# A post-norm decoder layer on one core: the first block's rows are stored as f16 parts and come back transposed by a DMA, where TensorE transposed them before

## The chip, the cores and the metric

The kernel runs on one core of a Trainium2 chip. The metric is the device time of one launch in microseconds (us), the median of three runs. The core has five engines that run side by side and meet only at semaphores: TensorE (PE in the rows; PEld is its weight load), VectorE (DVE), ScalarE (ACT), GpSimd (POOL), and SyncE (SP), which here does nothing but issue DMAs. SP's DMAs all go onto one DMA queue, q1.

## The reference

Sixteen sequences of 112 rows and 1024 columns pass through three blocks; each is `layernorm(x + block(x))`.

```python
# self-attention, head size 256, biases on q, k, v and the output
qkv = einsum('bsc,cf->bsf', x, Wqkv) + bqkv
x = layernorm(x + softmax(q @ k.T / 16) @ v @ Wo + bo)                # called x1 below
# cross-attention over ctx (375 rows of 1024 for each sequence)
Q = x @ Wq.T + bq;  K = ctx @ Wk.T + bk
x = layernorm(x + softmax(Q @ K.T / 32) @ ctx)                        # x2
# feed-forward, 2752 wide, weights packed in 4 bits and unpacked with scales and zeros
x = layernorm(x + (silu(x @ Wg) * (x @ Wu)) @ Wd)
```

## The kernel before

**Precision.** An f32 operand of a large product is split into an f16 high part and an f16 rest, and the product is three f16 products (high x high, high x rest, rest x high). Splitting takes two instructions: ACT writes the scaled high part, and DVE writes "scaled value minus high part".

**Stages.** The 16 sequences (n, in code also m) go in 4 groups (g) of GB = 4 (b is the place in a group).

*Self-attention, 33 to about 250 us.* For each group PE makes the four q/k products (index f), which ACT copies out in order (L1083; banks 2 and 3 in turn, so f + 2 cannot start before f is copied), then values, scores and, after the softmax, the output product of each sequence. DVE adds the residual (L482), takes the statistics (L376, L379, L381), waits for POOL's inverse deviation (L950), and applies the norm (L386), which signals `s_n`. SP stores each finished row tile `yo[b % 2]` as x1 (L1707) and loads the residual rows of the sequence two further on (L1705); POOL adds the output bias to these (L959), a step that stands in its queue just ahead of the inverse deviation of the sequence before. This run of norms lies beside the next group's q/k products on PE. DVE begins the next group with a maximum over its input (L401) and, in groups 1 and 2, with a block of small table instructions, ahead of the softmax. `xtp` holds a group's transposed input in f16 parts.

*Weights of the cross-attention, about 240 to 354 us.* Wq and Wk are multiplied in f32, in eight chunks of some 13.7 us on PE (`m_chunk`). ACT copies each out (L1124) and, just ahead, issues the load of the Wq columns of the chunk after next. Beside the last two chunks stand the x1 transposes of group 0: `x1_transposed(m, b, bank)` loads nothing itself; it takes row tiles that SP and ACT loaded back from x1 into `xs3`, makes eight f32 transposes of 112x128 into two banks (L1385), and `x1t_hi` on ACT (L1132) and `x1t_lo` on DVE (L645) write two f16 parts of them each into `xtp`.

*Cross-attention, 390 to 745 us.* One pass of a loop per sequence n on PE: logits (112x375) with a quarter of the g products (`g_chunk`: x1 times the combined weight, for the pair of sequences after this one), context transposes (L1457), softmax transposes (L1475), another quarter, the attended product, the last quarter, the x1 transposes of sequence n + 4 (L1385), and the transposes of the finished x2 rows of n - 1 (L1490). Each quarter is copied twice by ACT (L1139, L1143) and split by POOL (L1024); the logits of an even n wait for the last of these splits. The first quarter after the logits of an odd n waits for `s_x1l`, the end of `x1t_lo`.

*Feed-forward, 745 to 1977 us.* Not touched.

Each engine's order is written out by hand, with `Fori` loops over groups; `Fori(1, NG - 1)` runs groups 1 and 2, groups 0 and 3 stand outside.

## Time and profile before

| | |
|---|---|
| median of 3 runs | 1975.22 us (1974.12 to 1978.18) |
| the profiled execution | 1978.52 us, of which the span from first to last instruction is 1976.8 us |
| PE | busy 1889.8 us (96% of the span), 11238 matmuls |
| DVE, ACT, POOL | busy 880.5 us (45%), 476.2 us (24%), 320.3 us (16%) |
| granted TensorE clock | mean 0.988 of 2.4 GHz |
| DMA | 157.07 MB, queue q1 takes 26.5% of the 16 engines' time |

The profile's page gives busy time by engine, the span in slices, the chain of work that ended last, and the costliest groups of instructions. A timeline shows the instructions of one engine in order of time, with the idle time before each and what ended it. PE is busy nearly throughout, so its few idle pieces show where another engine sets the pace. Every time in the rows below is from the one profiled execution.

### The profile page before, as it was taken

The page shows a single profiled execution, that of the slowest core. Times are in us where ns is not written, and L with a number is a line of the kernel's source. Part 1 is how long each engine was busy: PE and PEld are TensorE (multiplying, and loading weights), DVE is VectorE, ACT ScalarE, POOL GpSimd, SP SyncE. Part 2 cuts the span into 40 slices and gives each one's busy share as a digit, 9 for nine tenths or more (in the row PEclk, how much of TensorE's full clock was granted, in tenths as well). Part 3 has the DMA queues.
Part 4 walks back from the last instruction along what each step waited for, and adds up shares of the span by engine and source line. Part 5 has one row for each costly group of instructions (what it writes and reads, how often), then busy time and mean ns, then how long its engine had stood idle before and what let it go on. Part 6 is the DMA issues. An engine that isn't in the chain of part 4 may idle for free.

```text
span 1976.8 us, 28966 instructions
## 1 busy us (share of the span) xinstructions
PE 1889.8 (96%) x11238; PEld 1094.2 (55%) x11238; DVE 880.5 (45%) x1404; ACT 476.2 (24%) x788; POOL 320.3 (16%) x262
## 2 busy tenths in 40 slices
PE   4898999899999987999999999999999999999998
PEld 2666644688888863544544444444455444444443
DVE  5578512578878865344344434434434311111111
ACT  2221102566556542212122222222121200000000
POOL 0221285111111102111112111111111000000000
PEclk9999999999999988999999999999999999999999
DMA  9232441234344311212121122121121322221220
GB/s 304 82 107 69 115 136 57 75 104 134 120 120 132 119 54 35 54 39 43 39 53 43 34 58 43 34 58 34 43 52 35 84 102 90 101 101 52 99 101 21
DMA packets 142336, 157.07 MB, mean 79 GB/s; under 512 B 101817, under 2 KB 116345, under 8 KB 140093
## 3 DMA queue, kind: packets, MB, share of 16 engines
q1 hardware_dynamic: 135772, 152.07, 26.5%
q10 hardware_dynamic: 6496, 4.06, 0.8%
q8 instruction: 47, 0.77, 0.2%
q14 instruction: 21, 0.16, 0.0%
HBM read 112.64 MB, written 43.46 MB: 79 GB/s over the span
## 4 chain that ended last, share of the span: by engine, by line
PE 57%; issue 32%; DVE 6%; POOL 2%; ACT 1%; DMA 1%; POOLq 0%; SPq 0%; DVEq 0%; ACTq 0%
PE psum L1303 54%; POOL arena L1024 1%; DMA arena<-in_x 1%; PE psum L1457 1%; PE psum L1574 1%; PE psum L1296 1%; PE psum L1592 1%; DVE arena L834 1%; POOL small L950 0%; DVE small L401 0%; DVE arena L394 0%; DVE arena L482 0%; DVE arena L714 0%; POOL arena L959 0%; DVE small L376 0%
## 5 line engine op out<-in xcount | busy, mean ns | idle before, releaser
L1303 PE MATMUL psum<-arena 128*128 128x448 f16 (+9 forms) x9432 | 1751.9, 347 | 26.3 <-POOL arena L1024 6.5
L1303 PEld LDWEIGHTS psum<-arena 128*128 128x128 f16 (+5 forms) x9432 | 972.5, 106 | 781.1 <-issue 96.6
L1049 POOL TENSOR_TENSOR arena<-arena 128x1024 f16<-128x1024 f32 (+1 forms) x65 | 139.1, 2140 | 685.9 <-ACT arena L1246 685.9
L890 DVE SCALAR_TENSOR_TENSOR arena<-psum,small,arena 128x448 f32<-128x448 f32 x84 | 57.4, 684 | 418.3 <-PE psum L1303 418.3
L930 DVE SCALAR_TENSOR_TENSOR arena<-psum,small,arena 128x512 f32<-128x512 f32 x28 | 21.0, 751 | 333.2 <-PE psum L1303 321.5
L1246 ACT ACTIVATE arena<-arena 128x1024 f16<-128x1024 f32 (+1 forms) x65 | 68.7, 1057 | 270.4 <-DVE arena L876 270.4
L950 POOL TENSOR_TENSOR small<-small 112x1 f32<-112x1 f32 (+1 forms) x46 | 25.5, 554 | 614.0 <-DVE small L381 613.9
L1259 ACT ACTIVATE arena<-arena 128x448 f16<-128x448 f32 (+1 forms) x88 | 50.7, 576 | 291.9 <-DVE arena L890 291.9
L1149 ACT ACTIVATE arena<-psum 128x750 f16<-128x750 f16 x96 | 72.0, 809 | 64.4 <-PE psum L1457 64.4
L874 DVE TENSOR_TENSOR arena<-arena,psum 128x1024 f32<-128x1024 uint32 x65 | 79.4, 1221 | 2.6
L896 DVE TENSOR_TENSOR arena<-arena 128x448 f16<-128x448 f32 (+1 forms) x88 | 55.0, 625 | 57.1 <-ACT arena L1259 57.1
L876 DVE TENSOR_TENSOR arena<-arena,psum 128x1024 f32<-128x1024 f32 x65 | 79.3, 1220 | 2.2
L1024 POOL TENSOR_TENSOR arena<-arena 128x224 f16<-128x224 f32 x64 | 43.6, 681 | 183.2 <-ACT arena L1143 183.2
L1154 ACT ACTIVATE arena<-arena,small 128x1024 f16<-128x1024 f32 (+1 forms) x48 | 55.1, 1154 | 65.8 <-DVE small L710 65.8
L714 DVE SCALAR_TENSOR_TENSOR arena<-arena,small 128x1024 f16<-128x1024 f32 (+1 forms) x48 | 61.2, 1278 | 20.4 <-ACT arena L1154 20.3
L683 DVE TENSOR_REDUCE small<-arena 128x1 f32<-128x1024 f32 (+1 forms) x48 | 58.2, 1213 | 16.5 <-DMA arena<-in_ctx 16.5
L1253 ACT ACTIVATE arena<-psum,small 128x448 f32<-128x448 f32 (+1 forms) x88 | 54.7, 622 | 44.3 <-PE psum L1303 44.2
L376 DVE BATCH_NORM_STATS2 small<-arena 112x6 f32<-112x512 f32 (+1 forms) x92 | 58.7, 680 | 0.0
L859 DVE TENSOR_TENSOR arena<-arena,small 128x1024 uint32<-128x1024 uint32 x43 | 52.4, 1219 | 0.0
L386 DVE TENSOR_SCALAR arena<-arena,small 112x1024 f32<-112x1024 f32 (+1 forms) x46 | 39.9, 867 | 28.0 <-POOL small L950 28.0
L1457 PE MATMUL psum<-ident_f,arena 128*128 128x128 f16 (+1 forms) x768 | 49.1, 218 | 1.6 <-ACT arena L1149 1.1
L1457 PEld LDWEIGHTS psum<-ident_f,arena 128*128 128x128 f16 (+1 forms) x768 | 45.4, 97 | 3.8 <-ACT arena L1149 2.1
(187 smaller groups left out, 878.3 us busy)
## 6 DMA issues: line engine op xcount, KB each, us to landing
h_scratch<-arena SPq DMA_DIRECT2D x88, 224.0 KB, 2.9
arena<-h_scratch SPq DMA_DIRECT2D x13, 1408.0 KB, 6.1
arena<-in_ctx SPq DMA_DIRECT2D x32, 512.0 KB, 3.6
arena<-in_x SPq DMA_DIRECT2D x32, 448.0 KB, 5.5
x_scratch<-arena SPq DMA_DIRECT2D x32, 448.0 KB, 3.1
arena<-x_scratch SPq DMA_DIRECT2D x30, 448.0 KB, 4.0
arena<-in_L_ffn_down_qweight SPq DMA_DIRECT2D x21, 512.0 KB
arena<-in_ctx SPq DMA_DIRECT2D x16, 448.0 KB
```

Source lines behind the costliest of these rows:

```text
L376: dve.bn_stats(st[0:n, 6 * h:6 * h + 6], y[:, h * HALF:(h + 1) * HALF]).then_inc(s_st, 1)
L683: ins = dve.tensor_reduce(cmx[0:CP[c], c:c + 1], cx[0:CP[c], c, :], AX.X, ALU.max, apply_absolute_value=True)
L714: dve.scalar_tensor_tensor(cxp[b % 2][0:CP[c], 1, c, :], cx[0:CP[c], c, :], fc[0:CP[c], b:b + 1], cxp[b % 2][0:CP[c], 0, c, :], ALU.mult, ...
L874: dve.tensor_tensor(w, w.bitcast(U32), zeros, ALU.subtract).then_inc(s_dq, 1)
L876: dve.tensor_tensor(w, w, scales, ALU.mult).then_inc(s_wf, 1)
L890: dve.scalar_tensor_tensor(h_f[0:n, :], up[0:n, :], sc_u[0:n, :], g_act[0:n, :], ALU.mult, ALU.mult).then_inc(s_hf, 1)
L1024: pool.tensor_tensor(gtp[:, 1, y, t], g_f, gtp[:, 0, y, t], ALU.subtract).then_inc(s_gl, 1)
L1049: pool.tensor_tensor(dst[1], src, dst[0], ALU.subtract).then_inc(s_wl, 1)
L1149: act.activation(cxt[:, :, c, :], bkh[ct_bank[c % 4]][:, :, 0:CTX], ACT.Identity).then_inc(s_cta, 1)
L1246: act.activation(dst, src, ACT.Identity).then_inc(s_wh, 1)
L1303: mm = pe.matmul(out, a, r, start=(k == 0), stop=(k == len(pairs) - 1))
L1457: mm = pe.transpose(bkh[ct_bank[c % 4]][:, l, r * P:r * P + CP[r]], cxp[b % 2][0:CP[r], l, r, c * P:(c + 1) * P], ident_h[0:CP[r], 0:CP[r]])
```

## The change

Each finished x1 row tile is split while it is still in SBUF. ACT writes the high part (`x1_hi`, 112x1024, f32 in, f16 out), DVE the rest (`x1_lo`), both into `x1p[b % 2]`, and SP stores both parts to a new DRAM tensor of f16 rows of 2048 (`store_parts`). `load_x1t` loads such a tile with a transposing DMA (the DMA crossbar) straight into the columns of `xtp`. Gone are the 128 PE transposes of x1, the 32 ACT and 32 DVE instructions on their results, and the 16 loads of x1 rows into `xs3`. New are 16 ACT and 16 DVE instructions of 112x1024, 16 stores of 448 KB and 16 transposing loads of 448 KB. `x1p` lies where the cross-attention later has its residual tiles.

The diff, with a line of context before each place:

```diff
@@ -67,6 +67,8 @@
     x2_d = nc.dram_tensor("x2_scratch", (NT, D), F32).ap()
+    x1p_d = nc.dram_tensor("x1_parts_scratch", (NT, 2 * D), F16).ap()
@@ -125,6 +127,7 @@
         g_f = carve(at_tab + 28 * P + 10 * D, [2 * S], F32)
+        x1p = carve(at_tab + 28 * P + 2 * D, [2, 2, D], F16)
@@ -152,7 +155,6 @@
         xr = carve(at_ctxt, [2, D], F32)
-        xs3 = carve(at_xs, [2, D], F32)
@@ -267,8 +269,9 @@
         s_gf = sem("group_factor_step"); s_ko = sem("output_factor")
-        s_x1t = sem("x1T_in_psum"); s_x1h = sem("x1T_hi_ready"); s_x1l = sem("x1T_lo_ready")
-        s_xs3 = [sem(f"x1_rows_in{i}") for i in range(2)]; s_xr3 = [sem(f"x1_residual_in{i}") for i in range(2)]
+        s_x1h = sem("x1_hi_ready"); s_x1l = sem("x1_lo_ready")
+        s_x1o = [sem(f"x1_parts_out{i}") for i in range(2)]; s_x1t = [sem(f"x1T_half{q}_in") for q in range(2)]
+        s_xr3 = [sem(f"x1_residual_in{i}") for i in range(2)]
@@ -361,6 +364,7 @@
                 dve.sem_inc(s_yout[i], 16)
+                dve.sem_inc(s_x1o[i], 16)
@@ -380,6 +384,12 @@
                 dve.tensor_scalar(ve[0:n, :], mv[0:n, 1:2], EPS, None, ALU.add).then_inc(s_eps, 1)
+            def x1_lo(n, b):
+                dve.wait_ge(s_x1h, n + 1)
+                dve.scalar_tensor_tensor(x1p[0:S, b % 2, 1, :], yo[0:S, b % 2, :], XS, x1p[0:S, b % 2, 0, :],
+                                         ALU.mult, ALU.subtract).then_inc(s_x1l, 1)
@@ -437,6 +447,8 @@
                     wo_split()
+                else:
+                    x1_lo(g * GB - 1, GB - 1)
@@ -476,12 +488,16 @@
                     dve.wait_ge(s_yout[b % 2], 16 * (2 * g + b // 2 + 1))
+                    if not known(n, 2):
+                        dve.wait_ge(s_x1l, n - 1)
                     norm_stats(yo[0:S, b % 2, :], n, s_y, 2 * n + 1)
+                    if b:
+                        x1_lo(n - 1, b - 1)
@@ -637,15 +653,6 @@
             self_attention(NG - 1, False, (select,))
-            def x1t_lo(m, b, bank):
-                cols = slice(b * S, (b + 1) * S)
-                for j in range(2):
-                    dve.wait_ge(s_x1h, 2 * m + j + 1)
-                    dve.scalar_tensor_tensor(xtp[:, 1, 4 * j:4 * j + 4, cols],
-                                             bk[bank + j][:, 0:TG].rearrange("p (a t) -> p a t", a=4), XS,
-                                             xtp[:, 0, 4 * j:4 * j + 4, cols], ALU.mult, ALU.subtract).then_inc(s_x1l, 1)
@@ -774,8 +781,6 @@
                         context_lo(n + 2, (b + 2) % GB, 1)
-                    if more:
-                        x1t_lo(n + GB, b, 6)
@@ -794,17 +799,14 @@
                                               ALU.max, apply_absolute_value=True))
+            x1_lo(NB - 1, GB - 1)
             context_factor(0, 0, False)
-            x1t_lo(0, 0, 4)
-            x1t_lo(1, 1, 6)
             largest_of_m(0, 5, 0)
-            x1t_lo(2, 2, 4)
-            x1t_lo(3, 3, 6)
@@ -1076,12 +1078,20 @@
                     act.activation(xtp[:, 0, KC - 1 - k, :], bk[xt_bank[k % 4]][:, 0:TG], ACT.Identity, scale=fx).then_inc(s_xh, 1)
+            def x1_hi(n, b, filled):
+                act.wait_ge(s_n, n + 1)
+                act.wait_ge(s_x1o[b % 2], 16 * filled)
+                act.activation(x1p[0:S, b % 2, 0, :], yo[0:S, b % 2, :], ACT.Identity, scale=XS).then_inc(s_x1h, 1)
                                    bias=bqk[:, f:f + 1]).then_inc(s_qke, 1)
+                    if f == 0 and not known(g, 1):
+                        x1_hi(g * GB - 1, GB - 1, 2 * g)
@@ -1098,6 +1108,8 @@
                     x_hi(g + 1, range(KC // 2, KC))
+                for b in range(GB - 1):
+                    x1_hi(g * GB + b, b, 2 * g + b // 2 + 1)
@@ -1124,14 +1136,6 @@
                                psum[:, i * 1024:(i + 1) * 1024], ACT.Identity).then_inc(s_me, 1)
-            def x1t_hi(m, b, bank):
-                for j in range(2):
-                    act.wait_ge(s_x1t, 2 * m + j + 1)
-                    act.activation(xtp[:, 0, 4 * j:4 * j + 4, b * S:(b + 1) * S],
-                                   bk[bank + j][:, 0:TG].rearrange("p (a t) -> p a t", a=4),
-                                   ACT.Identity, scale=XS).then_inc(s_x1h, 1)
@@ -1188,26 +1192,16 @@
                         context_hi(n + 2, (b + 2) % GB, 1)
-                    if more:
-                        x1t_hi(n + GB, b, 6)
                         context_hi(n + 2, (b + 2) % GB, 2)
+            x1_hi(NB - 1, GB - 1, NB // 2)
                     m_chunk(e, i, True)
-            x1t_hi(0, 0, 4)
-            x1t_hi(1, 1, 6)
-            for i in range(2):
-                act.wait_ge(s_yout[i], 16 * (NB // 2 + 1))
-            for m in (2, 3):
-                act.dma_start(xs3[0:S, m % 2, :], x1_d[m * S:(m + 1) * S, :]).then_inc(s_xs3[m % 2], 16)
             m_chunk(KC // 2 - 1, 0, False)
-            x1t_hi(2, 2, 4)
-            x1t_hi(3, 3, 6)
@@ -1377,15 +1371,6 @@
             pe.wait_ge(s_wk, 48)
-            def x1_transposed(m, b, bank):
-                pe.wait_ge(s_xs3[b % 2], 8 * (m - b % 2) + 16)
-                for j in range(2):
-                    for a in range(4):
-                        mm = pe.transpose(bk[bank + j][:, a * S:(a + 1) * S],
-                                          xs3[0:S, b % 2, (4 * j + a) * P:(4 * j + a + 1) * P], ident[0:S, 0:S])
-                    mm.then_inc(s_x1t, 1)
@@ -1406,14 +1391,8 @@
             for i in range(2):
-                if i:
-                    pe.wait_ge(s_x1l, 4)
-                x1_transposed(2 * i, 2 * i, 4)
-                if i == 0:
-                    pe.wait_ge(s_cf, 1)
-                x1_transposed(2 * i + 1, 2 * i + 1, 6)
                 m_chunk(KC // 2 - 1, i)
-            pe.wait_ge(s_x1l, 2 * GB)
+            pe.wait_ge(s_cf, 1)
@@ -1496,8 +1475,8 @@
                     logits(n, b)
-                    if not known(n, 1):
-                        pe.wait_ge(s_x1l, 2 * (n + GB) if more else 2 * NB)
+                    if has(2) and b % 2 == 0:
+                        pe.wait_ge(s_x1t[1 - b // 2], 32 * (g + 1 + b // 2))
@@ -1523,9 +1502,6 @@
                         g_chunk(4 * (b % 2) + 3, 1 - b // 2)
-                    if more:
-                        pe.wait_ge(s_y3, 2 * (n + 1))
-                        x1_transposed(n + GB, b, 6)
@@ -1535,6 +1511,7 @@
             context_t(0, 0)
+            pe.wait_ge(s_x1t[0], 32)
@@ -1695,6 +1672,16 @@
                     sp.dma_start(xs[0:S, b, :], rows(x_rows, g * GB + b)).then_inc(s_xs[b], 16)
+            def store_parts(n, s):
+                sp.wait_ge(s_x1l, n + 1)
+                sp.dma_start(rows(x1p_d, n), x1p[0:S, s, :, :].rearrange("p l d -> p (l d)")).then_inc(s_x1o[s], 16)
+            def load_x1t(m, b):
+                sp.dma_start_transpose(xtp.rearrange("p l k t -> p (l k) t")[:, :, b * S:(b + 1) * S],
+                                       rows(x1p_d, m)).then_inc(s_x1t[b // 2], 16)
@@ -1705,9 +1692,12 @@
                     sp.dma_start(rows(x1_d, g * GB + b), yo[0:S, b % 2, :]).then_inc(s_yout[b % 2], 16)
+                    if b or not known(g, 1):
+                        store_parts(g * GB + b - 1, (b + 1) % 2)
             load_group(1)
-            with sp.Fori(0, NG - 2) as g:
+            self_attention(0, True, True)
+            with sp.Fori(1, NG - 2) as g:
@@ -1734,15 +1724,16 @@
                          z_bf[1]).then_inc(s_tabo, 16)
+            for i in range(2):
+                sp.wait_ge(s_x1o[i], 16 * (GB // 2 + 1))
+            sp.wait_ge(s_v, 2 * NG)
+            for m in range(GB):
+                load_x1t(m, m)
                 sp.wait_ge(s_yout[i], 16 * (NB // 2 + 1))
-            def load_rows(m, b):
-                sp.dma_start(xs3[0:S, b % 2, :], rows(x1_d, m)).then_inc(s_xs3[b % 2], 16)
@@ -1766,34 +1757,32 @@
                     load_ctx(n, c)
-            for m in range(2):
-                load_rows(m, m)
             next_ctx(0)
+            store_parts(NB - 1, (NB - 1) % 2)
             sp.dma_start(tab_d[64:64 + GD, :], dtab_d[3 * GD:, :]).then_inc(s_tin[2], 16)
+            for i in range(2):
+                sp.wait_ge(s_x1o[i], 16 * (NB // 2 + 1))
             next_ctx(1)
-            for m in range(4, 6):
-                sp.wait_ge(s_x1t, 2 * m - 2)
-                load_rows(m, m % 2)
                     n = g * GB + b
+                    if loop and b % 2 == 0:
+                        sp.wait_ge(s_g, KC + 4 * n)
+                        for k in range(2):
+                            load_x1t(n + GB + k, b + k)
                         next_ctx(n + 3)
-                    if loop or n + 6 < NB:
-                        sp.wait_ge(s_x1t, 2 * n + 10)
-                        load_rows(n + 6, (b + 2) % GB)
@@ -1814,9 +1803,8 @@
                                      tabr_d[:, lo:hi, bass.ds(i * P, w)].rearrange("m g c -> g m c")).then_inc(s_tc[s], 16)
-            with sp.Fori(0, NG - 2) as g:
+            with sp.Fori(0, NG - 1) as g:
                 cross_attention(g, True)
-            cross_attention(NG - 2, False)
```

ACT at the seam between two groups of self-attention. Before, the next group's four q/k copies (L1083) follow the last copies of the transposed input (L1077):

```order
L1076 REGISTER_ALU
L1077 ACTIVATE arena<-psum,small 128x448 [waits xT_in_psum]
L1112 REGISTER_ALU
L1112 COMPARE_AND_BRANCH
L1083 ACTIVATE arena<-psum,small 128x448 [waits qk_in_psum,group_factor_step]
L1083 ACTIVATE arena<-psum,small 128x448 [waits qk_in_psum] x3
```

Now (L1079 is the old L1077, L1091 the old L1083, L1085 is `x1_hi`):

```order
L1079 ACTIVATE arena<-psum,small 128x448 [waits xT_in_psum]
L1084 REGISTER_ALU [waits rows_normalised]
L1085 ACTIVATE arena<-arena 112x1024 [waits x1_parts_out0]
L1085 ACTIVATE arena<-arena 112x1024 [waits x1_parts_out1,rows_normalised]
L1084 REGISTER_ALU [waits rows_normalised]
L1085 ACTIVATE arena<-arena 112x1024 [waits x1_parts_out0]
L1124 REGISTER_ALU
L1124 COMPARE_AND_BRANCH
L1091 ACTIVATE arena<-psum,small 128x448 [waits qk_in_psum,group_factor_step]
L1085 ACTIVATE arena<-arena 112x1024 [waits x1_parts_out1,rows_normalised]
```

Three high parts stand ahead of the first q/k copy and the fourth ahead of the second, each behind `rows_normalised` (`s_n`).

PE at the end of sequence 1 and the start of sequence 2 of the cross-attention, before:

```order
L1303 MATMUL psum<-arena 128x224 x24
L1385 MATMUL psum<-ident,arena 128x112 [waits x1_rows_in1,sum3_ready]
L1385 MATMUL psum<-ident,arena 128x112 x7
L1490 MATMUL psum<-ident,arena 128x112 [waits rows_normalised]
L1490 MATMUL psum<-ident,arena 128x112 x7
L1303 MATMUL psum<-arena 112x375 [waits g_lo_ready]
L1303 MATMUL psum<-arena 112x375 x23
L1303 MATMUL psum<-arena 128x224 [waits ctx_factor_step,g_copied,x1T_lo_ready]
```

and now (L1297 is the old L1303, L1469 the old L1490):

```order
L1297 MATMUL psum<-arena 128x224 x24
L1469 MATMUL psum<-ident,arena 128x112 [waits rows_normalised]
L1469 MATMUL psum<-ident,arena 128x112 x7
L1297 MATMUL psum<-arena 112x375 [waits g_lo_ready]
L1297 MATMUL psum<-arena 112x375 x23
L1297 MATMUL psum<-arena 128x224 [waits ctx_factor_step,g_copied,x1T_half0_in]
```

The eight x1 transposes are gone, and the g product waits for the transposing load instead of DVE.

SP at the start of the last group of self-attention, behind the stores of the tables (L1733, L1735). Before:

```order
L1733 DMA table_scratch<-arena 64x344 x2
L1735 DMA down_table_scratch<-arena 128x168
L1705 DMA arena<-in_x 112x1024 [waits sum_ready]
L1707 DMA x_scratch<-arena 112x1024 [waits rows_normalised]
L1705 DMA arena<-in_x 112x1024 [waits sum_ready]
L1707 DMA x_scratch<-arena 112x1024 [waits rows_normalised] x3
```

Now (L1692 is the old L1705, L1694 the old L1707):

```order
L1725 DMA down_table_scratch<-arena 128x168
L1682 DMA_TRANSPOSE arena<-x_parts_scratch 128x16x112 [waits v_in_psum,x1_parts_out1,x1_parts_out0]
L1682 DMA_TRANSPOSE arena<-x_parts_scratch 128x16x112 x3
L1692 DMA arena<-in_x 112x1024 [waits sum_ready]
L1694 DMA x_scratch<-arena 112x1024 [waits rows_normalised]
L1678 DMA x_parts_scratch<-arena 112x2048 [waits x1_lo_ready]
```

Four transposing loads stand ahead of the last group's residual loads, and each x1 store is followed by a store of parts.

## Rows read from the trace of the kernel before

**Rows 1.** PE's waits over the whole span: total us, times, longest.
```profile
PE psum L1346 <- DVE arena L456: 11.0, 2, 6.7
PE psum L1303 <- POOL arena L1024: 6.5, 7, 1.8
PE psum L1303 <- DVE arena L645: 2.4, 6, 1.1
```

**Rows 2.** PE timeline, cross-attention, sequences 3 to 5: start, us, instructions, [idle before <-releaser].
```profile
477.88 0.93 PE L1385 MATMUL psum<-ident,arena 112*128 112x112 f32 x8
478.65 1.05 PE L1490 MATMUL psum<-ident,arena 112*128 112x112 f32 x8
480.42 6.35 PE L1303 MATMUL psum<-arena 128*112 128x375 f16 x48 [0.71 <-POOL arena L1024]
...
502.28 4.01 PE L1303 MATMUL psum<-arena 128*112 128x375 f16 x24
506.55 2.47 PE L1303 MATMUL psum<-arena 128*128 128x224 f16 x24 [0.27 <-DVE arena L645]
```

**Rows 3.** PE timeline, end of sequence 13, where no x1 transposes stand.
```profile
704.64 1.05 PE L1490 MATMUL psum<-ident,arena 112*128 112x112 f32 x8
707.17 4.05 PE L1303 MATMUL psum<-arena 128*112 128x375 f16 x24 [1.48 <-POOL arena L1024]
```

**Rows 4.** PE timeline, first pass after sequence 0, and the loop's way back.
```profile
416.50 2.47 PE L1303 MATMUL psum<-arena 128*128 128x224 f16 x24 [1.12 <-DVE arena L645]
...
571.79 8.01 PE L1303 MATMUL psum<-arena 128*112 128x375 f16 x48 [2.03 <-issue]
```

**Rows 5.** PE timeline, the first x1 transposes and the product chunk behind them.
```profile
323.09 1.70 PE L1385 MATMUL psum<-ident,arena 112*128 112x112 f32 x16
324.62 13.91 PE L1303 MATMUL psum<-arena 128*128 128x512 f32 x32
```

**Rows 6.** ACT timeline, third q/k copy of groups 1 and 3.
```profile
105.48 0.72 ACT L1083 ACTIVATE arena<-psum,small 128x448 f32<-128x448 f32 x1 [3.82 <-PE psum L1303]
...
208.65 0.72 ACT L1083 ACTIVATE arena<-psum,small 128x448 f32<-128x448 f32 x1 [3.82 <-PE psum L1303]
```

**Rows 7.** DVE timeline, norms of sequences 3, 5, 7 and 11.
```profile
103.17 0.81 DVE L386 TENSOR_SCALAR arena<-arena,small 112x1024 f32<-112x1024 f32 x1 [0.66 <-POOL small L950]
...
142.03 2.83 DVE L386 TENSOR_SCALAR arena<-arena,small 112x1024 f32<-112x1024 f32 x1 [3.27 <-POOL small L950]
...
153.68 0.81 DVE L386 TENSOR_SCALAR arena<-arena,small 112x1024 f32<-112x1024 f32 x1 [1.25 <-POOL small L950]
...
204.65 0.81 DVE L386 TENSOR_SCALAR arena<-arena,small 112x1024 f32<-112x1024 f32 x1 [0.66 <-POOL small L950]
```

**Rows 8.** POOL timeline: bias added to the residual rows of sequence 4.
```profile
100.25 2.35 POOL L959 TENSOR_TENSOR arena<-arena 112x1024 f32<-112x1024 f32 x1 [1.64 <-DMA arena<-in_x]
```

**Rows 9.** Groups of instructions by shape: busy us, mean ns of one.
```profile
L714 DVE SCALAR_TENSOR_TENSOR arena<-arena,small 128x1024 f16<-128x1024 f32 x32 | 40.9, 1280 | 19.8 <-ACT arena L1154 19.7
L1154 ACT ACTIVATE arena<-arena,small 128x1024 f16<-128x1024 f32 x32 | 36.5, 1146 | 65.8 <-DVE small L710 65.8
```

**Rows 10.** DMA issues: count, KB each, median us from issue to landing.
```profile
h_scratch<-arena SPq DMA_DIRECT2D x88, 224.0 KB, 2.9
...
arena<-in_x SPq DMA_DIRECT2D x32, 448.0 KB, 5.5
x_scratch<-arena SPq DMA_DIRECT2D x32, 448.0 KB, 3.1
...
down_selection_scratch<-arena SPq DMA_DIRECT2D x1, 704.0 KB, 11.5
```

**Rows 11.** SP, DVE, ACT timelines, last group: residual load, last norm, second chunk's copy.
```profile
233.68 0.34 SPq L1705 DMA_DIRECT2D arena<-in_x  x1
...
249.93 1.41 DVE L386 TENSOR_SCALAR arena<-arena,small 112x1024 f32<-112x1024 f32 x1 [0.66 <-POOL small L950]
...
269.07 1.02 ACT L1124 ACTIVATE arena<-psum 128x1024 f32 x1 [12.57 <-PE psum L1303]
```

## The prediction

> **What bounds the kernel now.** I read the busy shares first (table above): PE is busy 96% of the span, the others under half. So what counts is PE's own work and the few places where PE waits. Its waits by releaser come next [rows 1]: in self-attention it waits for DVE twice before the softmax transposes, 6.7 us the longer time; in cross-attention for POOL's split of g before the logits of even sequences, 7 times, 6.5 us together, and for DVE's split of the x1 transposes, 6 times, 2.4 us. Then PE's timeline through a pair of sequences [rows 2] shows how these waits stand to the work that goes, and the timelines of ACT, DVE, POOL and SP at the seams of self-attention show what the new work lands on [rows 6 to 8, 11].
>
> **Removed in the cross-attention loop.** The eight x1 transposes start at 477.88 and the next block at 478.65: they cost PE 0.77 us a sequence, in 12 sequences [rows 2]. What becomes of it depends on what comes next.
> - Even to odd (6 times): the logits follow without a wait, so 0.77 us goes, and with it the wait for DVE's split at the next g product: 2.4 us in all, 1.12 in the first pass, some 0.26 after [rows 1, 2, 4]. 6 x 0.77 + 2.4 = 7.0 us. DVE's last context split ends about as early as PE then wants it, because DVE sheds two instructions ahead of it.
> - Odd to even (6 times): the logits wait for POOL's split of the last g quarter, and that chain (two copies on ACT, one split on POOL) starts at the end of the quarter, whatever PE does meanwhile. With x1 transposes, from 477.88 to 480.42 is 2.54 us, of which 0.71 us is a wait [rows 2]; at the end of sequence 13, without them, from 704.64 to 707.17 is 2.53 us, of which 1.48 is a wait [rows 3]. So the wait grows by what goes, and the saving is nil. The exception is the way back of the loop, where PE waits 2.03 us for nothing but its instructions [rows 4]; that starts 0.77 us earlier: 0.8 us.
>
> Loop: -7.8 us. ACT and DVE lose four instructions a sequence, which frees nobody else.
>
> **Removed beside the last weight chunks.** Sixteen transposes start at 323.09, the chunk behind them at 324.62: 1.53 us, twice, so 3.06 us [rows 5]. PE is continuous here, and the copies and splits taken off ACT and DVE let the next context tiles load earlier, so the chain behind moves up with PE: -3.1 us.
>
> A sentence of the skill bears on this. The trace gives 0.77/8 = 0.10 us for an f32 transpose of 112x128 in a run of eight [rows 2]. The Trainium skill, "VectorE: DVE Perf Modes", section "The three transpose paths", gives 390 ns for a 128x128 transpose on TensorE and 1309 ns for one through the DMA crossbar. By 390 ns the removal would be worth four times as much; the trace disagrees, and its number is used.
>
> **Added in self-attention.** Each high part costs ACT about 1.15 us and each rest DVE about 1.28 us (nearest rows: the same two operations on a context tile [rows 9]). DVE's rest of sequence n - 1 stands between the statistics and the norm of n, where DVE waits 0.66 to 3.27 us for POOL [rows 7], so at most 0.6 us of it shows. The store of parts adds 448 KB on the queue between the x1 store and the next residual load. I take 1.6 us for it, from what is left of the landing times (3.1 us a store, some 1.5 us of it latency [rows 10]); bounds are 0 (it fits into gaps) and 3.1 (a whole landing). The residual load feeds POOL's bias add, which starts as the load lands (100.25 [rows 8]), and the inverse deviation of the last sequence of a group queues behind that add. So a group's last norm comes later by 1.6 us or somewhat more. Then ACT makes that tile's high part (1.15 us) and only then copies q/k product 1 (0.72 us), for which product 3 waits on PE.
> - *Group 0 to 1.* Last norm ends at 103.98 [rows 7]; plus 1.6, plus 1.15 and 0.72 and hand-overs of 0.1, is 107.6. Product 3 could start when product 2 was done, 105.45 [rows 6]. PE loses 2.15 us. DVE is later by 1.6 + 1.28, and had about as much to spare. Bounds 1.2 (no queueing) and 3.5.
> - *Group 1 to 2.* Last norm 154.5. The stall at product 3 is 3 to 6 us, but PE waits 6.7 us later on for DVE [rows 1] and it vanishes there. What counts is DVE's chain: later norm (0.6 to 3.3 us) plus the rest of sequence 7 (1.28 us), less what comes back: the norm of sequence 5 took 2.83 us for 0.81 because it ran beside a POOL add [rows 7], and a later load moves that add away. Bounds -0.5 and +4.6; I take +1.3.
> - *Group 2 to 3.* Last norm 205.46, plus 2.35 (the waits here are only 0.66 us, so two rests show, and the load's 1.6), plus 1.97 is 209.8; product 2 ends at 208.6 [rows 6, 7]. PE loses 1.2 us. Bounds 0.2 and 3.
>
> Sum 4.65, say +4.7 us; bounds +0.9 and +11.1.
>
> **The transposing loads.** No row shows one. The nearest by size is the 448 KB store at 3.1 us; the nearest by its short runs is the h store, 224 KB in 2.9 us, whose runs are 256 bytes like the source rows of a 128-column block: twice its size, less the shared latency, is about 4.5 us. The far row is the selection store, 704 KB in 11.5 us, or 7.3 us for 448 KB [rows 10]. I take 3.5 us each in the stream. In the loop two are issued after an x2 store and wanted two sequences later, some 44 us (one takes 502.28 - 480.42 = 21.9 [rows 2]), and I estimate half a sequence, 11 us, before the context loads queue behind them, plus the 5 us by which these are early: hidden up to about 8 us each. In the last self-attention group four go out at about 226 us, ahead of the residual load of 233.7 [rows 11]. They take 14 us, until 240, so the last norm slips from 251.3 to about 254. ACT needs it before it issues the Wq load for the third chunk, which PE wants when the second ends, 269.0 [rows 11]: 17.7 us, less 1.15 for the split, about 3 (an estimate) for the POOL product that ACT also waits for, and 5.5 for a load [rows 10], leaves 8 us. Cost nil up to about 4.7 us each, then 4 us for every us more.
>
> The Trainium skill, "DMA: Bandwidth & Descriptors", section "Latency and other measured facts", puts the effective bandwidth of a DMA transpose at 261 GB/s; by that 448 KB would take an estimated 1.8 us and the sum would stay as it is. No run here shows it yet.
>
> **Sum.** -7.8 - 3.1 + 4.7 = -6.2 us. The profiled span goes from 1976.8 to 1970.6, that execution from 1978.52 to 1972.3. It stood 3.3 us above the median of 1975.22, so the median becomes **1969.0 us**. A measurement of this kernel tells about 0.2% (4 us) from no change.
>
> **Rivals.**
> - *The seams take it back.* The queue between x1 store, parts store and residual load is nearly full (the residual load's median is 5.5 us against 3.1 for a store [rows 10]), and ACT's in-order copies turn every us of a late norm into a PE stall. By the upper bounds +11.1 against -10.9: 1975.4 us. For: at each seam the last norm ends within 3.2 us of the end of product 2 [rows 6, 7]. Against: the 6.7 us wait of group 2 absorbs a stall. Chance 0.20.
> - *The seams cost little.* The store fits into gaps: +0.9 to +2, so 1965 us. Chance 0.08.
> - *The other side: slow transposing loads.* If each takes 7.3 us, the four hold up the last group's residual loads until 255, the last norm slips by 18 us, 10 more than the cover, and the net is +4 us; at 10 us each it is 21 more than the cover, net +15: 1979 to 1990 us. It decides from about 6.3 us each. For: short runs at both ends of the transfer. Against: the h stores with 256-byte runs keep pace. Chance 0.14.
> - *Tile by tile.* If a transposing load handles its 16 column blocks one after another at the time of a small DMA (1.3 us or more), it takes 20 us: the four block the queue for 80 us, and a pair in the loop takes 40 of the 44 us of two sequences and holds up the context tiles. At least 50 us more in self-attention: above 2020 us. The figure of 1309 ns named above points here. Chance 0.06.
>
> **How the numbers follow.** The forecast has 0.52, its own range 1965 to 1973. Eight in ten: down to 1964 (cheap seams) and up to 1983, the middle of the slow loads. Faster by over 0.2% (below 1971.3): 0.47 of the forecast, 0.05 of the first rival, 0.08 of the second, 0.60. Within 0.2%: 0.05 + 0.13 + 0.02 = 0.20. Slower: 0.02 + 0.12 + 0.06 = 0.20.
>
> **What the profile after would show.** In the loop, a pair of sequences in 1.0 us less than before, no wait for DVE's x1 split, and a wait of 1.5 us for POOL before every even logits. No gap between the last weight chunks. In self-attention, q/k copy 1 at 107 and 209 us, PE waits for ACT ahead of product 3 of about 2 and 1 us, and in group 2 one of 3 to 6 us with a shorter wait for DVE behind. The transposing loads land within 5 us each, and PE never waits for them. The prediction is wrong if their landing is over 6 us, if the even logits come earlier than 2.5 us after the last g quarter, or if residual loads land later by more than 3 us.

## The result: 0.29% slower, where a gain of 0.3% was forecast

| | kernel before | changed kernel |
|---|---|---|
| time, median of 11 runs each | 1975.55 us (1973.38 to 1978.68) | 1982.0 us (1979.53 to 1984.71) |
| ratio to before | | 1.0029, 95% interval 1.0020 to 1.0038 |
| profiled execution, its span | 1978.52, 1976.8 us | 1982.23, 1980.5 us |
| DMA packets | 142336 | 171519 |

The forecast was 1969.0 us, the range 1964 to 1983. The time fell into the range, near its top, and on the other side of no change. The two traces differ by 3.7 us, the medians by 6.4: the profiled execution of before stood 3.0 us above its median, that of the changed kernel 0.2. So these two traces show a smaller difference than the medians do.

Where the time went is read by laying PE's timelines side by side. A "seam" is the stretch in which DVE ends one group of self-attention (its norms) while PE makes the next group's q/k products and then waits for the softmax. First the kernel before (start, us, instructions, what ended the idle time): the out-projection of group 0, the softmax transposes of groups 1, 2 and 3, the last out-projection, the first logits of cross-attention, the end of the last g quarter before the loop's way back (x1 transposes, then x2 transposes), the start of the feed-forward part.

```profile
89.03 33.01 PE L1303 MATMUL psum<-arena 128*112 128x512 f16 x220 [0.91 <-DVE arena L482]
121.87 0.55 PE L1346 MATMUL psum<-ident,arena 112*112 112x112 f32 x4
176.17 0.99 PE L1346 MATMUL psum<-ident,arena 112*112 112x112 f32 x4 [6.74 <-DVE arena L456]
225.04 0.55 PE L1346 MATMUL psum<-ident,arena 112*112 112x112 f32 x4
230.06 15.29 PE L1303 MATMUL psum<-arena 128*112 128x512 f16 x59 [1.44 <-DVE arena L466]
...
390.43 6.32 PE L1303 MATMUL psum<-arena 128*112 128x375 f16 x48 [1.83 <-POOL arena L1024]
...
567.94 0.93 PE L1385 MATMUL psum<-ident,arena 112*128 112x112 f32 x8
568.71 1.05 PE L1490 MATMUL psum<-ident,arena 112*128 112x112 f32 x8
...
753.97 6.32 PE L1303 MATMUL psum<-arena 128*128 128x448 f16 x17 [3.55 <-POOL arena L1049]
```

The same view of the changed kernel, with the stalls between them and the loop's way back:

```profile
88.85 11.88 PE L1297 MATMUL psum<-arena 128*112 128x512 f16 x60 [0.90 <-DVE arena L496]
105.32 22.64 PE L1297 MATMUL psum<-arena 128*128 128x448 f16 x160 [4.60 <-ACT arena L1091]
127.80 0.55 PE L1340 MATMUL psum<-ident,arena 112*112 112x112 f32 x4
...
156.46 4.71 PE L1297 MATMUL psum<-arena 128*128 128x448 f16 x24 [2.21 <-ACT arena L1091]
162.40 16.76 PE L1297 MATMUL psum<-arena 128*128 128x448 f16 x136 [1.23 <-ACT arena L1091]
183.67 1.00 PE L1340 MATMUL psum<-ident,arena 112*112 112x112 f32 x4 [4.51 <-DVE arena L468]
...
236.44 0.55 PE L1340 MATMUL psum<-ident,arena 112*112 112x112 f32 x4
241.46 38.03 PE L1297 MATMUL psum<-arena 128*112 128x512 f16 x112 [1.45 <-DVE arena L478]
280.20 55.20 PE L1297 MATMUL psum<-arena 128*128 128x512 f32 x128 [0.71 <-DMA arena<-in_L_xattn_Wq]
335.46 27.63 PE L1297 MATMUL psum<-arena 128*128 128x512 f32 x64
...
399.61 6.32 PE L1297 MATMUL psum<-arena 128*112 128x375 f16 x48 [1.83 <-POOL arena L1026]
442.50 2.77 PE L1297 MATMUL psum<-arena 128*112 128x375 f16 x16 [1.48 <-POOL arena L1026]
...
571.66 1.05 PE L1469 MATMUL psum<-ident,arena 112*128 112x112 f32 x8
575.52 1.45 PE L1297 MATMUL psum<-arena 128*112 128x375 f16 x4 [2.81 <-issue]
579.15 7.25 PE L1297 MATMUL psum<-arena 128*112 128x375 f16 x44 [2.18 <-issue]
...
757.91 2.42 PE L1297 MATMUL psum<-arena 128*128 128x448 f16 x6 [3.55 <-POOL arena L1051]
```

- Seams: the changed kernel is 0.2 us ahead at the out-projection of group 0, then 5.9, 7.5 and 11.4 us behind at the softmax transposes and 11.4 at the last out-projection. So the three seams cost 6.1, 1.6 and 3.9 us, 11.6 together; +4.7 was forecast.
- Last weight chunks: they run in one piece of 27.63 us from 335.46, where before held two pieces with transposes between [rows 5]. That is the forecast -3.1. A wait for a weight chunk at 280.20 takes 0.7 us back. The loop starts 9.2 us late.
- Loop: from 399.61 to 757.91 is 358.3 us, before 363.5: -5.2 where -7.8 was forecast. The pairs are as forecast: no wait for DVE's split [rows 1, 4], 1.48 us for POOL before even logits (1.35 in later passes) where it was 0.71 [rows 2]. The way back is not: two stalls with 4 products between them and a slow stretch behind, where before had one stall [rows 4]. From the end of the last g quarter to the context transposes behind the quarter's logits it takes 14.58 us (571.66 to 586.24), before 11.70 (567.94 to 579.64): +2.9 where -0.8 was forecast. So the rest of the loop gave -8.1 where -7.0 was forecast.
- The sum of the trace: +11.6 + 0.7 - 3.1 - 5.2 - 0.3 (small shifts elsewhere) = +3.7 us.

Why the seams cost so much is seen where DVE, POOL and ACT work beside each other. The same timeline, engines mixed, tiles 1 to 3 of group 0 (L380 the statistics, L385 their last step, L390 the low part, which is the rest of the split, L396 the norm, L952 POOL's inverse deviation of 112 numbers, L961 its bias add, L1085 the high part, L1091 the copy of a q/k product; the other instructions are left out):

```profile
90.91 2.35 POOL L961 TENSOR_TENSOR arena<-arena 112x1024 f32<-112x1024 f32 x1 [3.62 <-DMA arena<-in_x]
91.11 3.23 DVE L390 SCALAR_TENSOR_TENSOR arena<-arena 112x1024 f16<-112x1024 f32 x1
93.22 1.53 POOL L952 TENSOR_TENSOR small<-small 112x1 f32<-112x1 f32 x1
94.72 2.34 POOL L961 TENSOR_TENSOR arena<-arena 112x1024 f32<-112x1024 f32 x1
94.79 2.83 DVE L396 TENSOR_SCALAR arena<-arena,small 112x1024 f32<-112x1024 f32 x1 [0.45 <-POOL small L952]
...
100.58 1.21 DVE L390 SCALAR_TENSOR_TENSOR arena<-arena 112x1024 f16<-112x1024 f32 x1
100.75 1.46 POOL L952 TENSOR_TENSOR small<-small 112x1 f32<-112x1 f32 x1 [3.68 <-DVE small L385]
102.24 0.81 DVE L396 TENSOR_SCALAR arena<-arena,small 112x1024 f32<-112x1024 f32 x1 [0.44 <-POOL small L952]
103.59 1.06 ACT L1085 ACTIVATE arena<-arena 112x1024 f16<-112x1024 f32 x1 [4.89 <-DMA x_parts_scratch<-arena]
104.29 1.28 DVE L380 BATCH_NORM_STATS2 small<-arena 112x6 f32<-112x512 f32 x2
104.56 0.71 ACT L1091 ACTIVATE arena<-psum,small 128x448 f32<-128x448 f32 x1
104.67 2.35 POOL L961 TENSOR_TENSOR arena<-arena 112x1024 f32<-112x1024 f32 x1 [2.47 <-DMA arena<-in_x]
105.95 0.15 DVE L385 TENSOR_SCALAR small<-small 112x1 f32<-112x1 f32 x1
106.02 2.08 DVE L390 SCALAR_TENSOR_TENSOR arena<-arena 112x1024 f16<-112x1024 f32 x1
108.54 0.81 DVE L396 TENSOR_SCALAR arena<-arena,small 112x1024 f32<-112x1024 f32 x1 [0.44 <-POOL small L952]
```

POOL's add ends at 93.26; the low part that began 0.2 us after it ends 1.08 us later, at 94.34. POOL's inverse deviation, which before took 0.55 us, ends 0.41 us behind the low part, at 94.75. I read from this that neither runs while the other does: the low part waits out the add, the small POOL instruction waits out the low part, and the norm waits for that. At 106.02 it is the same: the add of 104.67 ends at 107.02, the low part 1.08 us later, at 108.10. Beside no add the low part takes 1.21 us (100.58), and the statistics of 104.29 take 1.28 us beside an add as without one, so not every DVE instruction is held up. The Trainium skill has this in "SBUF — State Buffer", section "SBUF: two separate sides": GpSimd instructions and those of DVE that have two SBUF inputs or use both of its ports share one pair of ports, "an exclusive lock, not a bandwidth split". This trace agrees: behind the add the low part needs 1.08 of its 1.21 us. The prediction did not weigh that rule, and it was the one that spoke against the change.

What this makes of a tile is seen at the last one of group 0. Before, from the last step of the statistics to the norm [rows 7] was 0.82 us:

```profile
102.35 0.15 DVE L381 TENSOR_SCALAR small<-small 112x1 f32<-112x1 f32 x1
```

Now it is 2.59 us (105.95 to 108.54). Over tiles 1 to 3 the gaps grow by 1.4, 0.4 and 1.8 us, and the norm of 94.79 takes 2.0 us longer beside an add. So the last norm of group 0 ends 5.4 us later (109.35 for 103.98), where the prediction had 1.6 or somewhat more, and the low part of the last tile, 1.22 us, stands behind it ahead of the softmax.

Busy time by engine over the seams (stretch, length, PE, PEld, DVE, ACT, POOL, clock, DMA share, GB/s), kernel before:

```profile
85.00:230.00 145.00, 133.19 (x871) 94.90 (x869) 101.44 (x234) 25.76 (x58) 35.81 (x27) 0.98 0.38 107
```

and the changed kernel:

```profile
85.00:241.00 156.00, 136.53 (x870) 96.00 (x868) 121.30 (x244) 37.59 (x70) 45.66 (x27) 0.97 0.46 135
```

DVE is busy 19.9 us longer; twelve low parts take 21.0 us of it, of which 14.5 would be their own time at 1.21 us each and 6.5 are stretch. DVE's waits for POOL before norms fall from 15.1 to 6.1 us, so 9.0 us are covered and 10.9 are not, close to the 11.6 us that PE loses.

### The profile page after: what moved, and what is told of

It reads as the page before. It is cut to its first block, busy times and chain, and to the rows that moved or that the text cites. A ratio compares the mean times of both kernels' runs of the same rounds, so it can differ in the third digit from the quotient of the medians.

```text
span 1980.5 us, 28683 instructions
## 1 busy us (share of the span) xinstructions
PE 1880.4 (95%) x11110; PEld 1083.2 (55%) x11110; DVE 891.8 (45%) x1388; ACT 478.0 (24%) x772; POOL 334.0 (17%) x262
## 2 busy tenths in 40 slices
DMA packets 171519, 164.41 MB, mean 83 GB/s; under 512 B 131000, under 2 KB 145528, under 8 KB 169276
## 4 chain that ended last, share of the span: by engine, by line
PE 55%; issue 32%; DVE 5%; POOL 3%; DMA 3%; ACT 1%; POOLq 0%; SPq 0%; DVEq 0%; ACTq 0%
PE psum L1297 52%; DMA arena<-in_x 2%; POOL arena L1026 1%; PE psum L1436 1%; POOL small L952 1%; PE psum L1551 1%; POOL arena L961 1%; PE psum L1290 1%; DMA x_parts_scratch<-arena 1%; PE psum L1569 1%; DVE arena L836 1%; DVE arena L496 0%; DMA arena<-in_L_xattn_Wq 0%; DVE small L411 0%; DVE arena L404 0%
## 5 line engine op out<-in xcount | busy, mean ns | idle before, releaser
L1297 PE MATMUL psum<-arena 128*128 128x448 f16 (+9 forms) x9432 | 1754.4, 347 | 42.0 <-ACT arena L1091 10.6
L1297 PEld LDWEIGHTS psum<-arena 128*128 128x128 f16 (+5 forms) x9432 | 974.2, 106 | 798.6 <-issue 100.2
L952 POOL TENSOR_TENSOR small<-small 112x1 f32<-112x1 f32 (+1 forms) x46 | 36.8, 801 | 607.2 <-DVE small L385 607.1
L380 DVE BATCH_NORM_STATS2 small<-arena 112x6 f32<-112x512 f32 (+1 forms) x92 | 58.7, 679 | 0.0
L396 DVE TENSOR_SCALAR arena<-arena,small 112x1024 f32<-112x1024 f32 (+1 forms) x46 | 39.9, 867 | 19.4 <-POOL small L952 19.4
L961 POOL TENSOR_TENSOR arena<-arena 112x1024 f32<-112x1024 f32 x16 | 38.9, 2429 | 51.7 <-issue 27.7
```

The costliest lines, as they stand in the source:

```text
L380: dve.bn_stats(st[0:n, 6 * h:6 * h + 6], y[:, h * HALF:(h + 1) * HALF]).then_inc(s_st, 1)
L961: pool.tensor_tensor(xr[0:S, b % 2, :], xr[0:S, b % 2, :], bo_b[0:S, :], ALU.add).then_inc(s_xb, 1)
L1297: mm = pe.matmul(out, a, r, start=(k == 0), stop=(k == len(pairs) - 1))
```

## The experiments

### Which part costs: the cross half, the stores, the splits

**The cross half alone.** Edit to the changed kernel: both splits and the parts stores go, and the transposing loads read constants.

```diff
-                    if b:
-                        x1_lo(n - 1, b - 1)
...
-                for b in range(GB - 1):
-                    x1_hi(g * GB + b, b, 2 * g + b // 2 + 1)
...
-                                       rows(x1p_d, m)).then_inc(s_x1t[b // 2], 16)
+                                       x1p_d[bass.ds(m, S), :]).then_inc(s_x1t[b // 2], 16)
...
-                        store_parts(g * GB + b - 1, (b + 1) % 2)
```

> The cross-attention half of the change alone: self-attention as in the kernel before (no splits, no parts stores); the transposing loads are issued at the same places, of the same size, but read a block of constants written once at the start, so the attention block's output is not the reference's. Theory (the seams in self-attention are what went wrong, the rest is as forecast apart from the loop's way back): end of self-attention as before (out-projection of the last group at 230.1 us, within 1 us), the span 8 to 11 us under the kernel before (1965 to 1968 us). If the transposing loads are what costs (their issue or their traffic), the gain is under 5 us, and PE shows waits for them or a later residual or context load. If the 3.65 us at the loop's way back belong to the cross half (its code or its transfers), they are there again beside 575 us minus the 9 us shift; if they were of that one execution, they are not.

Measured: 1969.27 us, ratio 0.9968 (0.9957 to 0.9980). The last out-projection starts at 229.34, the span is 1967.6. The stalls at the way back are there (2.85 and 2.31 us). The forecast had -10.9 us for this half; with +2.9 in place of -0.8 at the way back that is -7.2, and the timed ratio is worth -6.3. So the cross half alone is about what the forecast wanted, the loop's way back excepted.

**Stores without splits** (x1 is stored a second time at the same places):

```diff
+                    sp.dma_start(rows(x1q_d, g * GB + b), yo[0:S, b % 2, :]).then_inc(s_x1o[b % 2], 16)
```

> As the changed kernel, but without the two splits: each x1 tile is stored a second time (448 KB, into a second scratch) in place of its parts, and the transposing loads read a block of constants, so the output is not the reference's. It tells what the extra store traffic costs by itself. Theory A (ACT's copies of q and k wait behind the late high parts): nothing of the 12.4 us at the seams comes with the stores, the last out-projection starts at 230 to 232 us (before 230.1, changed 241.5), the time is within 2 us of the cross half alone. Rival C (the stores delay the residual loads and by them the bias adds): 4 us or more at the seams, start at 234 or later.

Measured: 1970.9 us, 0.9978 (0.9969 to 0.9988); last out-projection at 229.57. The extra 7 MB of stores move the last out-projection by 0.2 us against the cross half alone, and the time by 1.6 us, inside the spread: rival C (4 us or more) falls, and with it the prediction's 1.6 us of queueing for each group. These stores go out right behind the x1 stores, a little earlier than the parts do in the changed kernel.

**Splits without stores** (only the first two tiles' parts are stored):

```diff
-                    if b or not known(g, 1):
-                        store_parts(g * GB + b - 1, (b + 1) % 2)
+                    if b and known(g, 1) and b < 3:
+                        store_parts(b - 1, b - 1)
```

> As the changed kernel, but only the parts of the first two tiles are stored; both splits are made for all tiles, and ACT's high part no longer waits for a parts store to land. The transposing loads read the two stored tiles, so the output is not the reference's. Theory A says that ACT's two high parts behind the norm still sit ahead of q/k copies 1 and 2, but the wait for the landed store (4.89 us before one of them in the changed kernel) goes: the last out-projection starts at 235 to 239 us (changed 241.5). Rival B (the cost is the DVE split beside POOL, which stretches both): 240 to 242, since both splits are still there. If the waits for the stores were everything, 230 to 232.

Measured: 1979.08 us, 1.0026 (1.0016 to 1.0036); last out-projection at 242.73, even a little later than in the changed kernel (the traced execution took 1984.72, 5.6 above its median). This was nearer to rival B's number than to theory A's. The 4.89 us in which ACT waited for a landed store were mostly no loss: the norm that the same high part needs ended at 103.05 in the changed kernel, 0.5 us before the high part began.

**ACT in another order:**

```diff
-                    if f == 0 and not known(g, 1):
-                        x1_hi(g * GB - 1, GB - 1, 2 * g)
+                    if f in (1, 2) and not known(g, 1):
+                        x1_hi((g - 1) * GB + f + 1, f + 1, 2 * g)
...
-                for b in range(GB - 1):
+                for b in range(GB - 2):
```

> The changed kernel with ACT's instructions in another order: the high part of a group's third tile stands behind the second copy of q/k (f=1), that of the fourth behind the third (f=2); everything else is the same and all of the computation is done. Theory A (in-order ACT, its copies of q/k behind high parts that wait for a norm or a landed store): the two PE stalls at the third and fourth q/k product of each group go, 7 to 11 of the 12.4 us come back, the span is 1970 to 1974 us. Rival B (DVE's split itself lengthens the chain to the norms and the softmax): 0 to 3 us come back, the time is 1977 to 1981.

Measured: 1980.49 us, 1.0025 (1.0015 to 1.0034). My theory A falls. PE's timeline in this run:

```profile
89.06 33.01 PE L1298 MATMUL psum<-arena 128*112 128x512 f16 x220 [0.90 <-DVE arena L496]
126.94 0.99 PE L1341 MATMUL psum<-ident,arena 112*112 112x112 f32 x4 [4.87 <-DVE arena L468]
184.27 0.99 PE L1341 MATMUL psum<-ident,arena 112*112 112x112 f32 x4 [7.33 <-DVE arena L468]
```

All q/k stalls are gone (33.01 us without a break), and PE waits for DVE behind them instead: 4.87 and 7.33 us. The last out-projection starts at 240.03, so 1.4 us come back and 10.0 of the 11.4 stay. The stall that the profile put on ACT was not what bounded the seam. DVE was.

**High parts alone, low parts alone**, each added to the cross half without stores, the low part against a constant high part (the cut is from the run with low parts):

```diff
-                dve.wait_ge(s_x1h, n + 1)
+                dve.wait_ge(s_n, n + 1)
+                dve.wait_ge(s_x1o[b % 2], 32)
```

> The cross half alone, with ACT's high parts of all x1 tiles put back at the changed kernel's places, but no low parts on DVE and no parts stores (the transposing loads read constants, so the output is not the reference's). After the run with ACT's order changed, theory B is the likelier: DVE is what bounds the seams, its own work there rose from 101.4 to 121.3 us. By it the high parts alone cost little: last out-projection at 230 to 233 us (cross half alone 229.3, both splits 242.7), PE's stalls behind ACT's q/k copies at most 4 us in all, time within 3 us of the cross half alone (1969). By theory A (ACT's copies late) it starts at 235 or later.

> The cross half alone, with DVE's low parts of all x1 tiles put back at the changed kernel's places, computed against a constant high part; no high parts on ACT and no parts stores (output not the reference's). Theory B (DVE's own work bounds the seams): last out-projection at 237 to 243 us, PE's waits there name DVE and not ACT, the time 8 to 12 us above the cross half alone, 1977 to 1981. Theory A: at 229 to 233, the time at 1969 to 1972. Each low part is expected to take over 2 us where it lies beside POOL's bias add and 1.2 elsewhere.

Measured: high parts alone 1970.46 us, 0.9982 (0.9971 to 0.9992), last out-projection at 230.04, 0.7 us behind the cross half alone, the time 1 to 3 us above it: they cost little. Low parts alone 1980.51 us, 1.0025 (1.0016 to 1.0034), at 236.39 (7.0 us behind the cross half alone), and no wait names ACT's copies. The busy times of the low parts alone:

```profile
85.00:239.00 154.00, 137.93 (x888) 97.96 (x887) 121.26 (x248) 25.89 (x58) 45.07 (x27) 0.97 0.40 111
```

DVE's 121 us and POOL's 45 are those of the changed kernel; ACT's 25.9 is before's. The start is 0.6 us short of the range expected. From the first out-projection to the last it is 146.3 us (90.14 to 236.39), the cross half alone 138.5, the run with ACT's order changed, which has both parts, 151.0. By these traces low parts alone make 7.7 of 12.4 us. By the timed runs they make 11 of 12: their ratio to before is 1.0025, that of the cross half alone 0.9968, that of the changed kernel 1.0029. In the changed kernel DVE waits for a high part only once at the seams (1.7 us), so the low part's wait for ACT is not what is missing in that trace. At the first seam of the low parts alone no norm takes 2.83 us and two of the three low parts take 1.2 us, so there the adds fell otherwise than in the changed kernel. Over the profiled executions this stretch took 136.9 to 141.0 us in nine kernels without splits and 149.9 to 154.6 in five with both. So a difference of 1 or 2 us here says nothing, and the 11.6 us of the pair above can be put at 12 by the means of the runs with the same self-attention code (two of the kernel before, three of the changed one) and at 14 by those of all nine and five.

**The pair without POOL's bias adds:**

```diff
-                pool.tensor_tensor(xr[0:S, b % 2, :], xr[0:S, b % 2, :], bo_b[0:S, :], ALU.add).then_inc(s_xb, 1)
+                pool.sem_inc(s_xb, 1)
```

> The changed kernel without POOL's bias adds in self-attention (the output bias is left out, only its semaphore is counted), so that nothing large runs on POOL beside DVE there. If the splits cost their own DVE time alone, 1.2 us each, the low parts stay at 1.2 and the seams cost against the same kernel before as much as now (11 us). If the collision with POOL makes a good part of it, low parts beside the norms fall from 2 to 3.2 us to 1.2, the tiny inverse deviation on POOL from 1.5 to 0.55, and the last out-projection starts 3 to 6 us earlier against its partner without bias than the 11.4 us of the pair with bias.

> The kernel before without POOL's bias adds in self-attention (the output bias is left out): the partner of the run above. Expected: norms of 2.83 us at the third tiles fall to 0.8, the last out-projection starts 0 to 5 us before the 230.1 us of the kernel before.

Measured, one run each: 1965.59 and 1961.24 us. From the out-projection of group 0 to the last one the changed kernel takes 141.9 us (82.80 to 224.74), its partner 133.1 (82.04 to 215.18): 8.8 us apart, with the adds 11.6. The last out-projections are 9.6 us apart, with the adds 11.4, where a good part of the collision was to show as 3 to 6 us less: a miss. The low parts fall to 1.216 us mean from 1.748, but the inverse deviation stays at 1.27, since the low part alone holds it up. So an estimate for the collision with the adds is 2 to 3 us of the 11.6, hardly more than the spread of this stretch; the rest is the low parts' own time on DVE and the inverse deviation behind them, which no run takes apart (none takes the inverse deviation off POOL). The partner's last out-projection starts 14.9 us earlier than before's, three times what I expected: 7.0 us of that lie ahead of the out-projection of group 0 and 7.9 behind it. So the adds already cost the kernel before far more than the splits' collision with them.

### The loop's way back

**No transposing loads in the loop:**

```diff
-                    if loop and b % 2 == 0:
-                        sp.wait_ge(s_g, KC + 4 * n)
-                        for k in range(2):
-                            load_x1t(n + GB + k, b + k)
```

> The cross half alone without the transposing loads of the loop (every pass uses the first group's rows, which are constants; output not the reference's). It tells two things. The price of the loop's 12 transposing loads: if they are hidden, the time is within 1.5 us of the cross half alone and POOL's 1.48 us waits before the even logits stay. And the loop's way back (571.79 us in the kernel before, where PE lost 3.7 us against a quarter pass without one; 7.3 in the changed kernel and in the cross half alone): if it is the loop's transposing loads, it falls to 4 us or less; if it is the shorter body of PE's loop, it stays at 7.

Measured: 1970.1 us, 0.9970 (0.9958 to 0.9982), like the cross half alone. The loop's loads are hidden, and the way back has its two stalls (2.82 and 2.98 us) without them.

**32 semaphore instructions on PE ahead of the products of g**, in the changed kernel, in the kernel before, and 8 of them in the changed kernel:

```diff
+            for _ in range(32):
+                pe.sem_inc(s_pad, 1)
```

> The changed kernel with nothing else than 32 semaphore instructions on PE ahead of the products of g, as in the padded version. If what that version gained came from the place of the loop's body in PE's code and not from its pacing, the two stalls at the way back (2.81 and 2.18 us, and the slow clock after them) go here too: loop start to hidden-layer start falls from 358.3 to about 351 us, the time from 1982 to 1974 to 1976 us, no longer slower than the kernel before. If not, it stays at 1980 to 1984.

> The kernel before with the same 32 semaphore instructions at the same place. Its body stands elsewhere in the code, so the sign is open: its own 2.03 us stall and slow quarter (3.7 us in all) may go (1971 to 1973 us), stay (1975 to 1977) or be split in two as in the changed kernel (1978 to 1980). Together with the run above it tells how much of the difference between the two kernels is the change and how much the place of the loop in the code.

> The changed kernel with 8 of those semaphore instructions in place of 32. In it PE gets 4 products (9 instructions with their weight loads) at the way back before it stalls a second time. If instructions come in blocks with fixed bounds, 8 more ahead of the body leave one or no product before the second stall, which stays; if any padding at all removed the stalls, there is none here.

PE's timeline at the way back, changed kernel with 32:

```profile
568.80 1.05 PE L1470 MATMUL psum<-ident,arena 112*128 112x112 f32 x8
571.21 6.35 PE L1298 MATMUL psum<-arena 128*112 128x375 f16 x48 [1.35 <-POOL arena L1027]
```

and with 8:

```profile
574.33 1.05 PE L1470 MATMUL psum<-ident,arena 112*128 112x112 f32 x8
582.04 8.84 PE L1298 MATMUL psum<-arena 128*112 128x375 f16 x48 [6.65 <-issue]
```

Measured: with 32, 1975.37 us, 0.9996 (0.9987 to 1.0005): the stalls and the slow stretch behind them are gone, and the changed kernel is no slower than the kernel before. With 8, one run: 1987.01 us, one stall of 6.65 us, no product ahead of it, as expected if instructions come in blocks with a fixed bound some 9 instructions behind the body's start. The kernel before with 32: 1975.24 us, 1.0000 (0.9991 to 1.0009), its single stall stays (2.43 us). So the stalls hang on where the body lies in PE's code: 0, 8 and 32 instructions ahead of the same body give two stalls, one long one, and none. The change takes PE instructions out ahead of the loop and in it, and so moved the body to a worse place. That the stalls are the loading of instructions is my reading; no view shows it.

One number missed: from the first logits to the feed-forward part the changed kernel with 32 takes 354.1 us where 351 was expected. The 18 attended products that start at 713.74 us took 6.83 us in it and 5.66 in the changed kernel, but 4.07 in the kernel before with 32. And 2.8 us of its 6.7 us shorter span came at the seams, inside their spread; the timed medians are 6.6 apart.

The quarter behind the way back takes 7.25 + 1.45 us against 6.35. The granted clock (the number behind POOL's) was 1.00 from 570 to 575 us. Behind the first stall and around the second it was 0.56, so a good part of that stretch ran at 1.2 GHz and not at 2.4, and then 0.76:

```profile
575.00:580.00 5.00, 2.30 (x7) 1.47 (x8) 3.68 (x7) 1.02 (x1) 0.00 (x0) 0.56 0.61 215
580.00:585.00 5.00, 5.00 (x30) 3.94 (x29) 0.83 (x2) 0.00 (x0) 0.00 (x0) 0.76 0.26 88
```

### A version that beats both

**Splits beside the chunks of m.** From 255 to 335 us DVE was busy 14.9 of 80 us and ACT 7.5 in the changed kernel. The rows of x1 are read back there and split:

```diff
+            for n in range(3):
+                x1_hi(n)
+            for k in range(KC - 2):
+                m_chunk(k // 2, k % 2, True)
+                for n in range(3 * k + 3, min(3 * k + 6, NB)):
+                    x1_hi(n)
```

> A version that could beat both, with the whole computation done: the splits leave the attention seams. All 16 tiles of x1 are read back from the x1 scratch into four row buffers beside the chunks of m (255 to 350 us), where DVE was busy 14.9 of 80 us and ACT 7.5 of 80; there they are split, stored as parts (four parts buffers), and the first group is loaded transposed before the loop. If theory B is right: seams as in the kernel before (last out-projection at 229 to 231 us), m section 0 to 3 us under before, loop as in the changed kernel (-5.2): 6 to 9 us under before, 1966 to 1970 us. If DVE's low parts slow POOL's sums beside the chunks (POOL busy 68 of 80 us there) until PE waits for them, or row traffic delays the weight chunks, up to 8 us of it are lost there and it is 1970 to 1976. By theory A or C the seams are also clean, so this run tells whether the change can pay, not which of them is right.

Measured: 1972.97 us, 0.9988 (0.9978 to 0.9998). The seams are clean (last out-projection at 225.40), but in the traced execution (1978.18 us, 5.2 above the median) PE waits for a weight chunk:

```profile
286.38 44.13 PE L1298 MATMUL psum<-arena 128*128 128x512 f32 x96 [9.21 <-DMA arena<-in_L_xattn_Wq]
```

and the DMA engines are full there (share 1.05, the number before the last; 346 GB/s):

```profile
275.00:285.00 10.00, 2.17 (x6) 0.62 (x4) 5.78 (x4) 4.47 (x5) 7.96 (x5) 0.83 1.05 346
```

**Paced, and paced with the 32 instructions.** The same edit, with the splits spread over the chunks:

```diff
-                for n in range(3 * k + 3, min(3 * k + 6, NB)):
+                for n in range(at[k], at[k + 1]):        # at = (1, 3, 5, 8, 11, 14, NB)
```

> The version with the splits beside the chunks of m, now paced: its high parts stand 1 ahead of the first chunk's copy and then 2, 2, 3, 3, 3, 2 behind the copies of the chunks (before: 3 ahead and 3 behind each), so that the row and parts transfers spread from 255 to 335 us; all of the computation is done. In the unpaced run the 16 DMA engines were full from 255 to 295 us (346 to 364 GB/s) and PE waited 9.21 us for a weight chunk at 286 us, then they were at 0.12. If that burst is the cause, the wait falls to 0 to 2 us and the time to 1962 to 1968 us (unpaced 1973). If the low parts beside POOL's sums are what delays the weight chunks, 4 us or more of the wait stay: 1969 or more.

> The paced version with 32 semaphore instructions put on PE ahead of the products of g, where PE waits for DVE anyway, so that the body of the cross-attention loop starts 32 instructions further on in PE's code. Theory: PE's 2.8 and 2.2 us stalls at the loop's way back come from where the body lies in the blocks in which PE's instructions are fetched (in four kernels with the shorter code PE gets 4 products and then waits a second time; in the kernel before, once). Then the way back changes, to one stall or another split of the two, worth up to 3.5 us. If it is the transfers of that moment (the context loads), nothing changes: 2.8 and 2.2 again.

Paced, the 9.21 us wait is gone, but the median is 1976.17, 1.0011 (1.0002 to 1.0020), where 1962 to 1968 was expected: a miss. Its trace is the fastest execution (1973.27, span 1971.5) and explains a part. Behind the last weight chunks PE waits 3.96 us for DVE, which waits for the second context:

```profile
348.87 0.77 PE L1386 MATMUL psum<-ident,small 128*128 128x128 f32 x2 [3.96 <-DVE small L690]
```

The sums behind it run slowly (3.41 us for the first 16 products, which take 1.84 in the changed kernel), so from the last chunks to the first logits it is 72.4 us, in the changed kernel 64.2. The 2.9 us between this execution and the median stay open. Its stalls at the way back are 2.86 and 3.35 us. Padded, it takes 1966.29 us, 0.9963 (0.9950 to 0.9977), and from the first logits to the feed-forward part 350.8 us instead of 359.2. The wait for DVE behind the second context is 2.93 us in it.

**The second context ahead of the transposing loads** on SP's queue:

```diff
+            next_ctx(1)
             for i in range(4):
                 sp.wait_ge(s_x1o[i], 16 * (NB // 4))
...
-            next_ctx(1)
```

> The padded, paced version with the second context's loads ahead of the first group's transposing loads and residual loads on SP's queue (all of the computation is done). In the padded version DVE waited 4.03 us for that context at 345 us, PE 2.93 us behind it at 350 us, and the sums after it ran at the slow clock. Expected: those waits shrink to under 1 us, the loop starts at 385 to 388 us (390.2), the time is 1960 to 1964 us. If the transposing loads then land too late for the first product of g, PE waits there and nothing is won (1966).

Measured: **1963.08 us, 0.9938 (0.9925 to 0.9950)**, with the whole computation done. From the last chunks to the first logits it is 64.2 us again. PE's timeline, where the wait of 2.93 us stood:

```profile
322.02 27.63 PE L1299 MATMUL psum<-arena 128*128 128x512 f32 x64
349.49 0.39 PE L1387 MATMUL psum<-ident,small 128*128 128x128 f32 x2
349.71 1.84 PE L1403 MATMUL psum<-ones,arena 128*128 128x1 f32 x16
```

## Why the prediction was wrong, step by step

- *The loop's pairs.* Right: 44.0 us a pair from 442.50 to 486.50 against 45.06 before, no DVE wait, POOL's wait grown by what went.
- *The way back.* Forecast -0.8, measured +2.9 by the same bounds (11.70 to 14.58 us). Behind the x2 transposes it is 7.3 us more than the 6.35 of its products alone against 3.7, POOL's usual wait included; the 0.8 us of the removed transposes went as forecast. The step that failed is to take a stall for instructions as fixed and only earlier. The padded runs show that it hangs on where the body lies in the code, which the change moved.
- *Beside the last chunks.* Right, -3.1.
- *Seams, forecast +4.7, measured +11.6.* This step turned the sign. The failed sentence is that of DVE's rest standing where DVE waits for POOL, "so at most 0.6 us of it shows". The wait was for a POOL instruction that did not run beside the rest, so the rest delays what it was to hide behind: 1.21 us of DVE, then 0.4 more of POOL. The mean was 1.75 us at the seams for the 1.28 taken, and the last norm of group 0 came 5.4 us later where 1.6 us or somewhat more was taken. By seam the forecast was 2.15, 1.3 and 1.2 us, the two traces show 6.1, 1.6 and 3.9. So the first and the third term failed. The second is near by luck: this stretch took 54.3 us in the traced kernel before and 50.1 to 53.2 in the other eight without splits; against the cross half alone the seams cost 6.1, 5.4 and 2.5. Low parts alone give 6.6 at the second of them, so there DVE's chain bounds by itself.
- *The parts stores,* 1.6 us a group: nil within the spread. The stores without splits show it. No row shows the 1.5 us of latency that this term was worked out with.
- *ACT's high parts,* 1.15 us with a stall at product 3: they took 1.06 us, and stalls came (4.60, 2.21 and 1.23, 1.05 and 1.19 us), the larger one each time but the last at product 2, which needs copy 0, and that stands behind the third tile's high part; the prediction had no stall there. The copies began at 104.6 and 110.4 us. They were the visible wait, not the cause: taken away, 10 of the 11.4 us stayed.
- *The transposing loads.* Right: median 4.8 us from issue to landing, PE never waits for them. SP issued the four in 7.77 us from 236.70, and the residual load behind them went out at 245.08, 11.4 us after before's, as late as everything else there. By the 261 GB/s of the Trainium skill ("DMA: Bandwidth & Descriptors", "Latency and other measured facts") the transfer would be an estimated 1.8 us; no row shows transfer and latency apart.
- *The rivals.* "The seams take it back" had the place and, with its bound of +11.1, nearly the size, with 0.20 of the chance, and with the way back added it is the case that came. Its mechanism, a full queue and ACT's copies, was not the one that the runs show; so that it came out near is in part luck. Slow transposing loads did not come.
- *The range.* 1982.0 lies in it, but only because its top was held open for slow transposing loads.

## What to carry to other kernels

An idle stretch before a norm hides new work only if the engine it waits for can run beside that work; for DVE's two-input split and POOL it couldn't here. A wait in the profile names who came last, not who bounds: take it away in a run before building on it. When instructions are removed ahead of a loop, look at its way back, and pad before judging the change: padded alike, the two kernels take 1975.4 and 1975.2 us. One trace for each version can mislead by some us, so hold its span against the timed median first.

## What the hardware showed that was not expected

- Some DVE instructions and POOL's exclude each other: a DVE low part of 1.21 us takes up to 3.23 beside a POOL add, POOL's 0.55 us instruction 1.53 beside a low part, a norm of 0.81 takes 2.83. It works both ways: an add of 2.35 us that began 0.2 us behind a low part, at 219.38, took 3.26. DVE's statistics took 1.28 us beside an add as without.
- SP takes 7.77 us to issue four transposing loads of 448 KB, and 1.5 to 4.0 us each over all sixteen, median 2.1, against 0.35 for a plain load of the residual.
- The same loop, moved on by 32 instructions in PE's code, has nothing but POOL's 1.35 us at its way back; moved by 8 (one run) it loses 9.1 us there (from 575.4 to 590.9 us for a quarter of 6.35), unmoved 7.3.
